# Half blocks of a mixture of experts: rows stationary and weights moving in the way in, gated rows turned by TensorE, one weight's parts made a slot sooner

## The reference

```python
logits = x @ gate_w + gate_b
probs = softmax(logits)
top_w, top_idx = top_k(probs, 2)
top_w = top_w / sum(top_w)
combine = zeros((T, 8)).at[arange(T)[:, None], top_idx].set(top_w)
h = silu(einsum('td,edf->tef', x, w1)) * einsum('td,edf->tef', x, w3)
out_e = einsum('tef,efd->ted', h, w2)
out = einsum('ted,te->td', out_e, combine)
```

## Time and profile before

| | |
|---|---|
| median of three runs | 2077.61 us |
| the profiled execution | 2078.52 us |
| its span, first to last instruction | 2076.8 us |
| TensorE busy | 1896.8 us (91%) |
| VectorE busy | 1550.3 us (75%) |
| ScalarE busy | 1149.3 us (55%) |
| experts' slots (first weight matmul to the end) | from 1408.6 us on |
| mean granted clock of TensorE | 0.969 |

### The profile page before, as it was taken

One profiled execution on the slowest core, in us unless ns is written; L12 is line 12 of the kernel. 1 busy time (PEld: TensorE's weight loads), 2 busy tenths in 40 slices (PEclk: granted clock), 3 DMA queues, 4 the chain that ended last, 5 costly groups with the idle time before them and its releaser, 6 DMA issues. The chain is left out here.

```text
span 2076.8 us, 35512 instructions
## 1 busy us (share of the span) xinstructions
PE 1896.8 (91%) x12100; PEld 1340.9 (65%) x12100; DVE 1550.3 (75%) x3240; ACT 1149.3 (55%) x2414; POOL 928.8 (45%) x672
## 2 busy tenths in 40 slices
PE   5899999986889999998999999939999999999998
PEld 3566677664543434343434343439999999999998
DVE  7999999982566777676767778547877776777775
ACT  2456666655346555555555555516665565656664
POOL 6999999981633335253434341112222231222222
PEclk8899999997999999999999999969999999999999
DMA  5222222300515142424242441036767666666662
GB/s 175 113 92 113 110 93 113 123 21 10 126 46 122 47 107 67 107 69 108 80 98 87 95 113 44 32 97 228 238 228 239 226 226 210 219 227 230 232 229 89
DMA packets 138569, 271.47 MB, mean 131 GB/s; under 512 B 13243, under 2 KB 90255, under 8 KB 132498
## 3 DMA queue, kind: packets, MB, share of 16 engines
q1 hardware_dynamic: 127916, 243.63, 37.4%
q0 software_dynamic: 9952, 25.25, 3.3%
q10 hardware_dynamic: 518, 0.27, 0.0%
HBM read 200.12 MB, written 70.47 MB: 130 GB/s over the span
## 5 line engine op out<-in xcount | busy, mean ns | idle before, releaser
L1472 DVE CUSTOM_DVE_ANT_0 x_dump<-x_ps,x_bias_q 128x512 bf16<-128x512 f32 x512 | 353.2, 690 | 103.7 <-PE x_ps L1156 90.7
L1341 ACT ACTIVATE x_PT<-x_ps 128x512 f32<-128x512 f32 x512 | 292.7, 603 | 230.0 <-PE x_ps L1171 226.5
L2017 ACT ACTIVATE X<-m_ps 128x256 f32<-128x256 f32 (+1 forms) x312 | 114.1, 366 | 221.7 <-PE m_ps L1949 218.2
L1156 PE MATMUL x_ps<-x_KS,x_QS 96*128 96x512 bf16 x512 | 199.1, 389 | 23.2 <-DVE x_mx L1472 22.5
L1915 POOL DMA_INDIRECT out_dram<-e_y,e_label x71 | 71.4, 1006 | 320.5 <-DVE e_y L2077 310.7
L1170 PE MATMUL x_ps<-x_bias_k,x_ident_b 128*128 128x512 bf16 x512 | 196.7, 384 | 2.1 <-DMA x_QS<-x_rows 1.0
L1171 PE MATMUL x_ps<-x_QS,x_KS 98*128 98x512 bf16 x512 | 196.6, 384 | 0.0
L1949 PE MATMUL m_ps<-e_x_lo,m_hi 128*128 128x256 f32 (+1 forms) x640 | 180.5, 282 | 5.9 <-issue 4.4
L1949 PE MATMUL m_ps<-e_x_hi,m_lo 128*128 128x256 f32 (+1 forms) x640 | 180.4, 282 | 0.0
L1949 PE MATMUL m_ps<-e_x_hi,m_hi 128*128 128x256 f32 (+1 forms) x640 | 180.4, 282 | 0.0
L2059 DVE TENSOR_TENSOR X<-X,m_ps 128x256 f32<-128x256 f32 (+1 forms) x312 | 114.3, 394 | 85.9 <-ACT X L2017 81.1
(11 more groups left out here) (332 smaller groups left out, 5417.5 us busy)
## 6 DMA issues: line engine op xcount, KB each, us to landing
m_raw<-in_L_ffn_w_dram SPq DMA_DIRECT2D x117, 1024.0 KB, 5.0
expert_in<-a_blank SPq DMA_DIRECT2D x34, 1032.0 KB, 4.3
parts<-x_part SPq DMA_DIRECT2D x24, 512.0 KB, 3.8
m_x<-expert_in SPq DMA_DIRECT2D x32, 258.0 KB, 5.1
next_mask_k<-in_maskT_dram SPq DMA_DIRECT2D x32, 256.0 KB, 2.7
next_mask_q<-in_mask_dram SPq DMA_DIRECT2D x29, 256.0 KB, 2.9
x_KS<-parts SPq DMA_DIRECT2D x16, 384.0 KB, 11.2
x_QS<-parts SPq DMA_DIRECT2D x8, 576.0 KB, 6.7
```

Source lines behind the costliest of these rows:

```text
L1156: pe.matmul(ps_max[m % 2], QS[b % 2][0:HROWS, h, q * P:(q + 1) * P], KS[b % 2][0:HROWS, h, :], start=True, stop=True).then_inc(s1_ps, 1)
L1341: act.activation(PT[unit % 2][:, k, :], ps_st[e % 3], ACT.Exp, scale=DH ** -0.5).then_inc(exp_done, 1)
L1472: dve.tensor_tensor_reduce(out=dump[:, :], in0=ps_max[m % 2], in1=bias_q[b % 2][:, q, :], scale=1.0, scalar=NEG, op0=ALU.add, op1=ALU.max, ...
L2017: act.activation(silu[f % 2][:, 0:wide], ps_h[f % 4][:, 0:wide], ACT.Silu).then_inc(silu_done, 1)
```

## The change

In a half slot, the way in is written by rows: the block's 128 rows are stationary and 512 columns of w1 or w3 move, so that there are 2 x 2 x 2 x 3 = 24 matmuls in place of 96. The results then have rows on partitions and hidden numbers along the free axis. Silu and gate are done on 512 hidden numbers at a time (2 instructions each in place of 8). The way out needs hidden numbers on partitions, so TensorE turns the gated rows with 8 transposes (`turn_gated`), after the next rows' `turn` and ahead of `project`. Their high and low parts are read from PSUM, 4 groups at a time (2 instructions each in place of 4).

The weights' parts move as well. Weight 0 of the slot after a half slot is split at the end of the slot ahead of the half one; weight 1 at the start of the half slot; weight 2 at its end (on ScalarE; on VectorE it was there before). Full slots are otherwise as they were.

```diff
+HALF_FF = FF // 2
@@ tensor
                     pe.wait_ge(x_lo_done, j + 1)
+                    if tiles_in(q) == 1:
+                        hidden_by_row(p)
+                        return
...
+                def hidden_by_row(p):
+                    for h in range(2):
+                        for n in range(2):
+                            for c in range(KC):
+                                mm = three_passes(ps_h[2 * h + n], [x[p][:, c, 0:P] for x in (x_hi, x_lo)],
+                                                  [w[p][n][:, c, h * HALF_FF:(h + 1) * HALF_FF] for w in (w_hi, w_lo)], c == 0, c == KC - 1)
+                        mm.then_inc(h_ps, FC // 2)
+                def turn_gated(j):
+                    for h in range(2):
+                        pe.wait_ge(gated_done, FC * j + FC // 2 * (h + 1))
+                        for f in range(FC // 2):
+                            mm = pe.transpose(ps_h[h][:, f * P:(f + 1) * P], wide_gated[h][:, f * P:(f + 1) * P], ident_f[:, :])
+                        mm.then_inc(g_turned, 1)
                 def project(i, q):
                     j, p, tiles = at_slot(i, q), q % 2, tiles_in(q)
+                    if tiles == 1:
+                        turn_gated(j)
@@ scalar
+                def hidden_by_row(i, q):
+                    j, p = at_slot(i, q), q % 2
+                    high_part(act, j + 1, 1 - p, 1)
+                    act.wait_ge(gated_done, FC * j)
+                    for h in range(2):
+                        act.wait_ge(h_ps, FC * j + FC // 2 * (h + 1))
+                        act.activation(wide_silu[h], ps_h[2 * h], ACT.Silu).then_inc(silu_done, FC // 2)
+                    for h in range(2):
+                        act.wait_ge(g_turned, 2 * (len(HALVES) * i + halves_before(q)) + h + 1)
+                        act.activation(g_hi[:, 4 * h:4 * h + 4, 0:P], ps_h[h].rearrange("p (f n) -> p f n", n=P), ACT.Copy)\
+                            .then_inc(g_high, FC // 4)
...
+                def following_parts(i, q):
+                    j, p = at_slot(i, q), q % 2
+                    x_high(i, q + 1)
+                    if tiles_in(q) == 1:
+                        high_part(act, j + 1, 1 - p, 2)
+                    if tiles_in(q + 1) == 1:
+                        high_part(act, j + 2, p, 0)
...
@@ vector
+                def gate_by_row(j, p):
+                    low_part(dve, j + 1, 1 - p, 1)
+                    for h in range(2):
+                        dve.wait_ge(silu_done, FC * j + FC // 2 * (h + 1))
+                        dve.tensor_tensor(wide_gated[h], wide_silu[h], ps_h[2 * h + 1], ALU.mult).then_inc(gated_done, FC // 2)
+                    for h in range(2):
+                        dve.wait_ge(g_high, FC // 2 * j + FC // 4 * (h + 1))
+                        dve.tensor_tensor(g_lo[:, 4 * h:4 * h + 4, 0:P], ps_h[h].rearrange("p (f n) -> p f n", n=P),
+                                          g_hi[:, 4 * h:4 * h + 4, 0:P].bitcast(F32), ALU.subtract).then_inc(g_parts, FC // 4)
...
                     low_part(dve, at_slot(i, q) + 1, 1 - q % 2, 2)
+                    if tiles_in(q + 1) == 1:
+                        low_part(dve, at_slot(i, q) + 2, q % 2, 0)
                     add_y(i, q)
```

More of the change, by code:

```diff
@@ L1860, in experts @@
             gated = [X[:, 2 * n + 2:2 * n + 4, :] for n in range(2)]
+            wide_gated = [gated[n].rearrange("p t d -> p (t d)") for n in range(2)]
+            wide_silu = [X[:, 2 * n + 6:2 * n + 8, :].rearrange("p t d -> p (t d)") for n in range(2)]
             g_hi, g_lo = sb("g_hi", [P, FC, BLK], F32R), sb("g_lo", [P, FC, BLK], F32R)
@@ L1869, in experts @@
             silu_done, gated_done, g_parts = sem_("silu_done"), sem_("gated_done"), sem_("g_parts")
+            g_turned = sem_("g_turned")
             g_high, y_left, y_out = sem_("g_high"), sem_("y_left"), sem_("y_out")
@@ L2007, in gated_high @@
                     act.activation(g_hi[:, 2 * k:2 * k + 2, 0:wide], gated[k % 2][:, :, 0:wide], ACT.Copy).then_inc(g_high, 1)
+                def hidden_by_row(i, q):
[9 more added lines that the diff above has]
+                            .then_inc(g_high, FC // 4)
                 def hidden(i, q, following=True):
                     j, p, wide = at_slot(i, q), q % 2, tiles_in(q) * P
+                    if tiles_in(q) == 1:
+                        hidden_by_row(i, q)
+                        return
                     for f in range(FC):
@@ L2026, in _ @@
                     hidden(0, q)
-                    x_high(0, q + 1)
+                    following_parts(0, q)
                 with act.Fori(1, ROUNDS) as i:
@@ L2030, in _ @@
                         hidden(i, q)
-                        x_high(i, q + 1)
+                        following_parts(i, q)
                 for q in REST:
@@ L2034, in _ @@
                     if q + 1 in REST:
-                        x_high(ROUNDS, q + 1)
+                        following_parts(ROUNDS, q)
             @block.vector
@@ L2052, in gate @@
                     j, p, wide = at_slot(i, q), q % 2, tiles_in(q) * P
+                    if tiles_in(q) == 1:
+                        gate_by_row(j, p)
+                        return
                     for k in range(FC // 2):
```

## The result

The changed kernel takes 2109.52 us (median of 4 runs, 2100.12 to 2114.98), the kernel before 2076.82 (4 runs, 2069.03 to 2078.5): a ratio of 1.0159, interval 1.0134 to 1.0183. The forecast was 2061.5 us and faster, with a range up to 2075. It is slower, by about twice what it was to gain. The profiled execution took 2112.5 us, with a span of 2110.7.

The account below looks back on a forecast made before the run. The prediction took TensorE to bound the kernel in the experts. It summed 22.6 (way in less tail) - 3.6 (rows' chain) - 3.0 (clock) = 16.0 us saved, giving 2061.5 us, ratio 0.992, range 2053 to 2075.

Parts of the forecast that it names:

- The way in: Half slot's TensorE matmuls: 24 with 512 columns at 0.224 us replace 96 narrow ones, saving 5.32 us per half slot.
- Rival D: Way in: 512-column fp32 matmuls stream at half rate, 0.46 us apart, so 2.4 us slower per half slot, 2095; chance 0.06.
- the prediction's 131 ns at 512 columns: Way in: the Trainium skill's sustained matmul gap, making the kernel another 16 us faster, about 2046; given 2 in 100.
- The tail: Half slot's end: the way out waits for silu, gate, transposes and parts formerly hidden, costing 2.09 us per half slot.
- `add_y` of the slot ahead: VectorE before the half slot: weight 0's low part goes ahead of it, moving its start 2.20 us later.
- The clock: TensorE behind the half slots' tails: two drops to half clock of 1.5 us each, 3 us lost in all.
- rival C: Clock halves behind every tail and into the next way in: no change, 2079, or 7 us faster, 2071; chance 0.11.
- the output rows' chain: Store, fetch, landing and `add_y` around half slots: nearly a tie, 0.6 us lost in six of seven, 3.6 in all.
- Rival B: Output rows' chain replaces TensorE as the bound: 2 to 3 us lost per half slot, 2069 to 2076; chance 0.13.

Follow-up runs that it names:

- the held load: Changed kernel with the last weight part's load issued only once the half slot's fetched rows have landed: 2099.54 us, ratio 1.0122 to the kernel before.
- the adding store: Changed kernel without fetches of output rows, GpSimd's store adding to the rows in DRAM instead: 2058.01 us, ratio 0.9913 to the kernel before.
- the moved parts: Kernel before with only the weights' parts moved, way in by columns as before: 2074.19 us, ratio 1.0029; four of ten runs took 2089.08 to 2095.34.

## Why the prediction was wrong

**What held.** The way in: predicted 24 x 0.224, measured starts 0.233 us apart (the 24 from 1561.94 to 1567.54 take 5.60 us, against 5.38); the half slot, from transposes to transposes, went from 16.59 to 11.51 us, a gain of 5.1 where 5.32 was computed. The mean duration of such a matmul is 395 ns, which answers to the earlier trace rows: that of the bf16 form (389), not 627. Rival D is excluded, and so are the prediction's 131 ns at 512 columns. The tail: predicted 2.09 us; with the chain removed, the slot behind the half one takes 16.88 us against 14.69, 2.2 more. VectorE's multiplication and low part took 685 and 691 ns, as the row had them. `add_y` of the slot ahead started 2.2 us later in its slot, as computed.

**The clock.** Three us were set aside for it, and rival C for more. Windows of the changed kernel (busy time of PE, PEld, DVE, ACT, POOL, then PEclk):

```profile
1567.50:1574.50 7.00, 6.02 (x49) 5.53 (x48) 3.41 (x6) 4.08 (x5) 1.29 (x2) 1.00 0.80 314
1583.00:1592.00 9.00, 7.87 (x46) 7.88 (x47) 7.01 (x11) 6.23 (x10) 2.85 (x1) 0.65 0.40 131
```

In the tail, with twelve transposes and gaps of 0.66 and 0.31 us, the granted clock stays at 1.00, the 2.4 GHz level: nothing lost, and rival C as it was put is wrong. The run without fetches has 1.00 from 1407 to 2020 us, over all seven tails. Of what the Trainium skill ("TensorE: Matmul & The Clock Gate", Part 4: PE-mode transpose) says, that transposes don't keep the clock up as matmuls do, these tails show no effect. Behind the 5.15 us wait it is 0.65 on average over 9 us. The slot's 24.71 us, less 16.88 without the chain and less the wait, leave 2.7 us for it. So the clock does take part, but as a follower of the new waits.

**The step that failed** is the term of the output rows' chain: "I take 0.6 us in six of the seven", with 2 us as its upper bound. Measured, the slot shown takes 24.71 us in place of 14.69 and the predicted 16.8: some 8 us, not 0.6; over the six it is 7.1 each (below). Its numbers were read from an undisturbed moment. The store takes 1.0 for its first instruction: it took 2.18, held by a low part, and the next fetch starts 5.53 us behind its end, not 4.75. The fetch "takes 1.05": it took 2.42, held. The rows land "3.6 us behind its end": 6.2, behind a load. These four, 1.2 + 0.8 + 1.4 + 2.6, account for the 5.8 us by which `add_y` is later than computed. And the lateness, which full slots were to "give back about 1 us each", was handed on and kept up by the same meetings. That GpSimd can be held could have been seen. In the trace of before, GpSimd's and VectorE's rows right behind the half slot are

```profile
1585.68 3.02 POOL L1907 DMA_INDIRECT e_y<-out_dram,e_label  x1 [6.44 <-DMA out_dram<-e_y,e_label]
```

```profile
1585.50 2.29 DVE L1748 TENSOR_TENSOR e_lo<-m_raw,e_hi 128x2048 fp32r<-128x2048 f32 x1
```

three times the duration of its neighbour in the earlier trace rows, and again an end (1588.70) 0.91 us behind that of the low part (1587.79). The forecast took the rows of 1569.98 and 1589.01 and left this one out, and with it the group's mean of 1408 ns. The landing too: where `add_y` waited in that trace, it started 3.6 us behind the fetch once, and 4.4 to 4.6 us the other times.

**Rival B** named the mechanism (the rows' chain takes the place of TensorE) but gave it 2 to 3 us per half slot and a total still faster than before. Its sign, gaps of over 1 us in the way in behind a half slot, is there in all seven. But no held instruction went into its price.

**The balance of the spans**, 2110.7 - 2076.8 = 33.9 us, from the starts of the rows' transposes on TensorE. The seven half slots take 35.5 us less (7 x 5.07). The slots behind six of them take 143.6 us in place of 87.8, 55.7 more; less 6 x 2.2 for the tail, which was foreseen, that is 42.5, or 7.1 each. The slot behind slot 19, which had the 4.40 us wait of the earlier trace rows, takes 2.8 more, the other full slots 14.1 more. That makes 37.1 for the experts; the stages ahead of them, which the change doesn't touch, were 3.2 shorter in this execution. By cause they are 40.5 of new waits, 15.4 for the seven tails and some 20 for the clock (its records give 25 us lost in the experts, before 5), less the 35.5 and the 4.4 of the old wait: 36, which leaves 1 us open.

**Open.** Why the rows come late behind a load that is sent out only 0.9 us ahead of the fetch's end wasn't looked into further; that they do, the held load shows. How the 51 us divide between held GpSimd instructions and rows behind a load isn't known: the adding store takes both away at once. Why the late state ends where it does wasn't tried, nor what the four long runs of the moved parts waited for, nor a version in which no low part can meet GpSimd; the semaphore tried here, raised by GpSimd's queue, didn't make one.

## What to carry to other kernels

When a slot gets shorter, every chain that crosses it (here: store, landing, fetch, landing, add) has to be added up anew with the durations that it has beside the work it will then meet, and the longest rows of an operation count as well as the typical one. Look also for two engines that wait for the same event: what they do next will coincide each time. A chain that passes its own lateness on has no small price: either it has a margin or it sets the pace. The cheapest repair was not another order but a link less, the store that adds in DRAM.

## What the runs showed of the hardware

- A GpSimd indirect transfer of 1.0 us that starts while VectorE subtracts two 128x2048 operands in SBUF ends 0.87 to 0.93 us behind the subtraction (41 times in the changed kernel, up to 3.1 us in all); one that adds, 1.55 us when free, ends 1.42 behind it (up to 3.46). A subtraction that starts inside a transfer did not lengthen it (1.05 us, before, 1569.98).
- A semaphore that GpSimd's queue raises behind an indirect transfer can come before the transfer's row: what waits for it started 0.17 us before that.
- Fetched rows (128 x 1 KB) are there 1.2 to 1.9 us behind the end of their issue where no weight load was sent shortly before (the held load); with a 1 MB load sent out 0.9 us ahead of that end it takes 5.0 to 6.2 us.
- Single-pass fp32 matmuls with 512 moving columns start 0.233 us apart, twice the 0.118 of 256 columns; with 128 columns they took 0.111.
- The granted clock stays at 1.00 through gaps of 0.3 to 0.7 us among transposes, and is 0.65 over the 9 us around and behind a wait of 5 us.
